# Three reduced-precision passes in place of full fp32 products, with operands split in two, in a fused attention and mixture-of-experts layer

## The reference

```python
x = L0_attn_hidden                                   # (4, 1024, 256)
x = x + attention(layernorm(x), Wq, Wk, Wv, Wo)      # window of 64 keys
x = x + ffn(layernorm(x), ...)

# ffn, xf = x as (4096, 256)
scores = sigmoid(xf @ gate_w.T + lb_bias)
topw, topi = top_k(scores, 2); topw /= topw.sum(-1) + 1e-8
for e in range(8):
    m = topi == e
    wmean = (topw * m).sum() / max(m.sum(), 1)
    y = (silu(xf @ gate[e].T) * (xf @ up[e].T)) @ down[e].T
    out += where(m.any(-1), y * wmean, 0)
out += (silu(x @ sgate.T) * (x @ sup.T)) @ sdown.T   # width 256, two halves
```

## Time and profile before

| what | value |
|---|---|
| median of 3 runs | 613.49 us (612.69 to 614.48) |
| profiled execution | 616.98 us, its span 615.2 us |
| PE busy | 555.0 us, 90% of the span |
| DVE, ACT, POOL busy | 354.0, 289.5, 218.4 us |
| chain that ended last, by engine | PE 71%, DVE 13%, an unknown queue 6%, ACT 4% |
| mean granted TensorE clock | 0.97 |

### The profile page before, as it was taken

How to read it: one execution, slowest core, us unless ns; L and a number is a source line. 1 busy time by engine, 2 the same in 40 slices (tenths; PEclk the granted TensorE clock), 3 DMA queues, 4 the chain that set the end, 5 groups by cost and what they waited for, 6 DMA issues and landing times.

```text
span 615.2 us, 14456 instructions
## 1 busy us (share of the span) xinstructions
PE 555.0 (90%) x4969; PEld 417.2 (68%) x4969; DVE 354.0 (58%) x1084; ACT 289.5 (47%) x650; POOL 218.4 (36%) x384
## 2 busy tenths in 40 slices
PE   7699999989898898898898987898999999999995
PEld 4466766666566565565575664786888887868884
DVE  4456577666465575675665567268555554533454
ACT  3366665645445555455455563221555554541110
POOL 4000012342240431422413423662456555555620
PEclk9899999999798998999999999698999999999999
DMA  7400000210201101112101101115455554518753
GB/s 249 164 3 3 2 2 4 62 45 20 63 23 40 52 20 55 37 27 63 36 2 38 36 2 38 70 57 159 135 152 162 153 159 134 157 58 301 247 147 126
DMA packets 37862, 50.79 MB, mean 83 GB/s; under 512 B 9244, under 2 KB 28063, under 8 KB 37792
## 3 DMA queue, kind: packets, MB, share of 16 engines
q1 hardware_dynamic: 31264, 33.02, 17.7%
q0 software_dynamic: 6528, 16.86, 8.3%
HBM read 27.36 MB, written 23.27 MB: 82 GB/s over the span
## 4 chain that ended last, share of the span: by engine, by line
PE 71%; DVE 13%; another core or an unknown queue 6%; ACT 4%; issue 3%; DMA 2%; POOL 1%; DVEq 0%; SPq 0%; POOLq 0%; ACTq 0%
PE ps L774 10%; PE ps L694 7%; PE ps L525 6%; PE ps L491 5%; PE ps L791 5%; PE ps L576 5%; PE ps L511 5%; PE ps L501 4%; DVE rmax L997 4%; PE ps L704 3%; PE ps L554 3%; PE ps L562 3%; PE ps L536 3%; PE ps L766 2%
## 5 line engine op out<-in xcount | busy, mean ns | idle before, releaser
L997 DVE TRANSPOSE_TENSOR_REDUCE rmax<-ps 128x32 f32<-128x1024 f32 x64 | 79.5, 1242 | 62.8 <-PE ps L525 61.0
L459 POOL DMA_INDIRECT y_rows<-vm,dest x72 | 70.2, 976 | 63.5 <-issue 40.1
L367 POOL TENSOR_TENSOR rstd<-mv,epsb 128x2 f32<-128x2 f32 x32 | 6.2, 193 | 241.6 <-DVE mv L982 241.6
L868 ACT ACTIVATE probs<-ps 128x1024 f32<-128x1024 f32 x64 | 65.7, 1026 | 25.0 <-PE ps L541 25.0
L774 PE MATMUL ps<-wF,wA 128*128 x288 | 75.0, 383 | 0.5 <-DVE wA L1246 0.5
L422 POOL DMA_INDIRECT z_slots<-z,slot x64 | 64.7, 1011 | 29.4 <-issue 18.0
L525 PE MATMUL ps<-bd,kT 64*128 64x256 f32 x512 | 66.4, 380 | 0.0
L694 PE MATMUL ps<-zT,wF 128*128 128x256 f32 x256 | 62.4, 388 | 0.6 <-ACT vm L957 0.6
L874 ACT COPY pvs<-ps 128x256 f32<-128x256 f32 x64 | 23.8, 372 | 81.5 <-remote 42.5
L694 PEld LDWEIGHTS ps<-zT,wF 128*128 128x128 f32 x256 | 49.5, 195 | 7.8 <-ACT vm L957 1.0
L525 PEld LDWEIGHTS ps<-bd,kT 64*128 64x128 f32 x512 | 50.0, 191 | 5.0
(11 more groups left out here) (160 smaller groups left out, 1095.5 us busy)
## 6 DMA issues: line engine op xcount, KB each, us to landing
z<-z_slots SPq DMA_DIRECT2D x72, 129.0 KB
bd<-y_rows SPq DMA_DIRECT2D x8, 512.0 KB, 7.4
out<-xs SPq DMA_DIRECT2D x16, 256.0 KB, 3.6
wF<-wffn SPq DMA_DIRECT2D x10, 384.0 KB, 3.3
xs<-x SPq DMA_DIRECT2D x7, 512.0 KB, 6.0
shift<-negs SPq DMA_DIRECT2D x128, 2.0 KB
z<-y_rows SPq DMA_DIRECT2D x4, 512.0 KB, 6.7
probs<-y_rows SPq DMA_DIRECT2D x4, 512.0 KB, 7.5
```

What stands on the lines that cost most here:

```text
L459: eng.indirect_dma_start(y_rows, bass.IndirectOffsetOnAxis(ap=dest[:, m:m + 1], axis=0), yo[:, m, :], None, bounds_check=K * T - 1, oob_is ...
L868: eng.activation(probs[:, n % 2, :], S[n % 2].rearrange("p a c -> p (a c)"), ACT.Exp, scale=HD ** -0.5).then_inc(s_P, 1)
L997: eng.tensor_reduce(rmax[:, n % 2, 0:32], S[n % 2].rearrange("p a (c q) -> p (a c) q", q=32), AX.X, ALU.max, apply_transpose=True).then_in ...
```

## The change

Every large product except `down` of the shared expert and the attention's inner products is made of three matmuls on operands of type fp32r, a 32-bit type that the matmul takes in reduced precision: hi x hi, hi x lo and lo x hi, where hi is the operand rounded to fp32r and lo the rest (`product`).

```diff
+                def product(out, lhsT, rhs, start, stop, skip=False):
+                    for n, (a, b) in enumerate(((0, 0), (0, 1), (1, 0))):
+                        mm = eng.matmul(out, lhsT(a), rhs(b), start=start and n == 0,
+                                        stop=stop and n == 2, skip_group_check=skip)
+                    return mm
```

```diff
-                    eng.tensor_copy(z1[:, m % 2, :], ps[:, 4 + m % 2, 0:D]).then_inc(s_z1, 1)
+                def rows_lo(t, q, m):
+                    eng.wait_ge(s_zh, t + 1)
+                    eng.tensor_tensor(z1[:, m % 2, 1, :], ps[:, 4 + m % 2, 0:D], f(z1[:, m % 2, 0, :]),
+                                      ALU.subtract).then_inc(s_zl, 1)
...
-                    chain(eng.tensor_tensor(table[0], const("tile").unsqueeze(2).to_broadcast([P, NTS, E]),
-                                           over_tiles(tiles_end), ALU.is_ge))
-                    chain(eng.tensor_reduce(tile_e[:, :], table[0], AX.X, ALU.add))
+                    chain(eng.tensor_scalar(fit, tiles_end, const("index"), None, ALU.is_le))
+                    chain(eng.tensor_reduce(e_col, fit, AX.X, ALU.add))
...
+                turn_of = [max(5 * g // 4 + 3, 2 * (g - GA) + 3) for g in range(NG)]
```

More of the change, by code:

```diff
@@ L294, in step @@
                             load_weights(g - 2)
+                        if n == 1 and old >= 2:
+                            store_zt(g - 2)
                 def prologue():
@@ L650, in step @@
                             yT_of(g + 2)
+                        if n == 0 and old >= 2:
+                            zT_of(g - 2, (place - 2) % GPB)
                         if project:
@@ L737, in epilogue @@
                     places_of(NG - 1)
+                    down(2)
+                    gate_up(5)
+                    eng.wait_ge(s_dg, 1)
+                    eng.matmul(ps[:, BANK_B, 64:64 + 2 * NTS], onesf[:, :], probs[:, 0, 64:64 + 2 * NTS],
+                               start=True, stop=True).then_inc(s_tb, 1)
+                    down(3)
                     gate_up(6)
@@ L790, in tile_down @@
                     after(eng, s_y1, t - 1)
[L791 to L792 removed]
+                    product(ps[:, 2 + m % 2, 0:D], lambda a: hT[:, m % 2, a, :],
+                            lambda b: weights(e, b, 4 * P, 6 * P), True, True).then_inc(s_d1, 1)
                 def tile(q, m, first, last):
@@ L1073, in step @@
                             normalise(1, g - 2, (place - 2) % GPB)
+                        if n == 1 and old == 3:
+                            comparisons(g - 3, last=False)
+                        if n == 3 and old:
+                            statistics(1, g - 1, (0,), False)
                         if ahead or n < BPG - 1:
@@ L1098, in step @@
                             normalise(1, g - 1, (place - 1) % GPB)
-                        if n == 2 and old:
-                            statistics(1, g - 1)
+                        if old or n:
+                            oT_lo(b - 1, (n - 1) % BPG)
+                        if n == 2 and g + 3 < NG:
+                            for c in range(2, XC) if old == 1 else ():
+                                eng.wait_ge(s_x[c], 16)
+                            statistics(0, g + 3, (0,), False)
                         if n == 3 and ahead and old >= 2:
```

516 lines of the change are left out of this document (333 added, 183 removed).

## The result

The changed kernel takes **633.4 us** (median of 4, 630.21 to 635.41) against 613.99 for the kernel before: ratio 1.031, 95% interval 1.026 to 1.036. It is slower by 3%, where 8% faster was forecast.

What follows compares the result with a forecast made beforehand. PE was taken to bound most of the kernel, apart from the sweep's unnamed hole and DVE's table in the epilogue. Terms -15 (tiles), -16 (sweep), -7.5 (epilogue), -11 (last stage) gave -49.5, from median 613.49 to 564 us; range 541 to 597.

Steps and rivals of the forecast that it cites:

- The unnamed hole: Sweep: ACT's unnamed wait while POOL scatters, 12 times, 42.5 us; taken as fixed, PE idling 0.3 us longer each.
- my own signs of being wrong: Whole kernel: a pass above 0.11 us, sweep steps that keep their length, or a growing hole in them.
- Tile stage: 72 tiles of three products: -15 us, from -23 to 0, a tile at 1.41 us.
- POOL runs without a gap and PE stalls: Rival, tile stage: a 1.35 us stall every four tiles, +24 us, so 588 us; chance 0.20.
- upper ends of my four terms: Worst cases of sweep (+15), tile stage (0), epilogue (-2) and last stage (-5).
- Price of a product: All 600 products: 0.327 us each instead of 0.432, saving 0.105 each, 63 us of PE time.
- slow pass: Rival, all 600 products: a product costs 0.648 us instead of 0.432, about 738 us in all; chance 0.08.
- Sweep: Sweep and prologue: -16 us, from -28 to +15; PE saves 1.66 us a step, a third lost to waits.
- DVE binds the sweep: Rival, sweep: it keeps its length, 0 instead of -16 us, so 580 us; chance 0.15.
- Epilogue: After the sweep: -7.5 us, from -10 to -2, by 44 cheaper products and a shorter DVE table.
- Last stage: Final stage: -11 us, from -12 to -5; 88 products save 9.2 us, three end additions becoming one save 1.8.

Runs made afterwards that it cites:

- e5: Kernel before with only its scatters' four indirect DMAs spread over four blocks; 587.36 us, ratio 0.958.
- e16: Kernel before, unaltered, profiled again; 613.02 us.
- e4: Changed kernel with each scatter's four indirect DMAs spread over four blocks; 577.27 us, ratio 0.937.
- e1: Changed kernel with one plain fp32 matmul on the hi parts in each product, lo parts made but unused; 625.56 us, ratio 1.019.
- e7: Changed kernel with the places and the scatter put ahead of the 1/std of y on POOL; 668.02 us.
- e12: e4 with a memset of 384 columns behind each tile-stage indirect DMA; 556.8 us beside a kernel before of 579.3 us.
- e2: Changed kernel with every indirect DMA replaced by a direct one of the same size to fixed rows, routing left out; 550.52 us.
- e3: Kernel before with every indirect DMA replaced by a direct one of the same size to fixed rows, routing left out; 578.62 us.
- e11: e4 with the first of PE's three table broadcasts moved behind a down and a gate_up in the epilogue; 575.62 us.
- e13: e12 with PE's last epilogue broadcast (tile weights) and DVE's copy of it moved behind the last down; 557.24 us beside 579.3 before.
- e17: e13 with a memset of 448 columns in place of 384; 560.43 us beside a kernel before of 578.8 us.
- e8: e4 with the tile stage's three products each one plain fp32 matmul of the hi parts; 565.08 us, ratio 0.920.
- e15: The kernel of e12 once more, beside a kernel before of about 614 us; 568.22 us, ratio 0.925.

## Why the prediction was wrong, by its own steps

**The unnamed hole (the step that failed).** I wrote that the hole in the sweep "is a fixed time" and that PE with less work idles longer in it, 0.3 us each. It costs 3.6 us a step before (24.45 against 20.87 in e5; 2.9 by e16's 23.75) and 5.3 us in the changed kernel (25.07 against 19.78 in e4). On twelve steps the difference is 20 us, or 29 by e16, where I had 4. Read at one clock (under e1) it has two parts. The first: at full clock the hold is worth 2.6 us before (23.45 against 20.87) and about 4.0 in the changed kernel (23.7 against 19.7), since the step does not shorten by what the passes save; nearly all of the 1.2 us becomes idle time and not 0.3. The scatter starts 10.15 us after the step in the changed kernel and in e1 alike, whatever a product costs, and in the kernel before at 9.3. So PE's products do not set when it starts, and the change has put 0.85 us on the way there, where I had 0.5. Which operation on that way does it was not shown; e7, which was to test it, did not. The second part is the clock, which my sum did not have at all: it fell in each of the changed kernel's nine steps, which makes 1.4 us a step on average, and in five of the kernel before's (two in e16), which makes 1.0 us (0.3). With it the sweep came out worse than without the change. I had put the hole down as something that the change leaves alone because its own rows, the indirect DMAs, are not touched. Of my own signs of being wrong all three came: a pass above 0.11, steps that keep their length, and PE's wait behind the hole, which grew from 22.3 to 39.0 us.

**Tile stage: the rival came.** "POOL runs without a gap and PE stalls" stood at +24 us for 0.20; the tile stage was to be at -15 + 24 = +9, and it is at +8.8. The place and the kind of stall were in the earlier trace rows; the chance was wrong. I set it against the sequencer that "keeps a tile above 1.4 us", but 1.42 us a tile is not enough: holds are still there at 1.58.

That the sum agrees to 0.2 us is luck. Against e12, which has no holds, they cost 19 us and not 24, and the base is not -15: without holds the stage is 108.3 us (e12) or 108.4 (e2), 10 less than the kernel before's and only 6 less than e3's 114.4. A tile takes 1.42 us, near my 1.41 but for the wrong reasons: a matmul is 0.119 us instead of 0.109, so nine of them and three transposes are 1.40, and the three REGISTER_ALU cost nothing visible. What I overlooked is that every eighth tile takes 2.1 to 2.3 us in e2 and in e12, always where PE's program loads the next eight expert numbers (`experts_of`); e3, whose kernel loads four at a time, has no tile over 1.9. No run changed this alone, so the cause is not shown.

**Two rivals from one cause.** I had kept the hole in the sweep and the stalls in the tile stage apart, one as a constant and one as a rival. Both go away with the same edit (e2) and come together. The upper ends of my four terms (+15, 0, -2, -5) add up to about 621 us, and to 645 with the stalls, and 633.4 lies between; I had cut the range at 597 because "not all come together". With one cause behind two of them they did.

**Price of a product.** 0.357 us where 0.327 was forecast: 45 us in all and not 63. The slow pass (0.648) did not come. My lower bound took the matmuls of the earlier trace rows to be at the lower clock, where the profile's window has 1.00, so it was no reading of a row. By an estimate from the Trainium skill ("FP8 and Floating Point Precision", TensorE Precision Notes: true FP32 is four passes) three passes would be 0.324; the row shows 0.357, so a reduced matmul of 256 columns is dearer than a quarter of the full product.

**Sweep without the hold.** -1.1 us a step had been forecast from 1.66 less a third for waits. The runs have 1.1 to 1.2 from 16 x 0.075 and no waits. "DVE binds the sweep" did not come: DVE is at 17.2 of 19.65 us in e2.

**Epilogue.** -7.5 became +5.5. Without indirect DMAs it is still +2.1 (51.9 against 49.8), so the holds are about 3.4 of it, as far as single executions tell: two of them stand in its chain in the changed kernel, the wait of 2.52 us and the 1.15 us of L672 below. For the rest, the table on DVE did get shorter, but PE must broadcast it in three pieces in its own order. Its chain in the changed kernel, where L810 and L823 are broadcasts:

```profile
400.11 2.52 another core or an unknown queue
...
419.54 1.15 PE ps L672
...
424.91 0.85 PE ps L810 x2
425.76 1.71 PE ps L773 x4
427.46 1.84 PE ps L530 x12
...
434.94 0.44 PE ps L823 x2
435.38 0.91 PE ps L773 x4
436.30 1.43 PE ps L530 x12
437.72 0.88 PE ps L773 x4
```

Before, the chain from 411 us on was DVE's alone; now it goes from DVE to PE and back, and ends in PE's own gate_ups and downs, the first of them at the lower clock (1.71 for a down in place of 0.87, 1.84 for a gate_up in place of 1.43; the granted clock is 0.52 from 424.9 to 428.4 us). Moving one broadcast (e11, e13, e17) did not clearly win anything back, so that the waits at the broadcasts make the 2.1 us is not shown.

**Last stage.** -9.8 where -11 was forecast: a pair is 2.30 us instead of 2.59, 22 x 0.29 = 6.4, and the rest is the shorter end, which e1 has too: with plain products its last stage is 3.5 us below the kernel before's. At 270 GB/s the chain of this stage still has no DMA in it.

**The version to keep.** e8 (565.1 us, 8.0% faster than the kernel before) leaves the lo parts out of the tile stage's products; e15 with all three passes is at 568.2, 7.5% faster. Both are mostly the spread scatter. Where no hold was, e12 is still 4% faster than the kernel before.

## What to carry to other kernels

An unnamed wait that comes with another engine's work is a suspect to be priced by a run, not a constant: ask what its length hangs on, and whether the engine that the change relieves sets the steps in which it stands. Making PE faster can bring everything else closer together, and in the sweep it was four indirect DMAs right behind each other that cost; spreading four of them over a step, a change of a few lines, gave 27 us before and 56 us after, more than the change of every product. And where one cause appears as two terms of a sum, their chances are not independent.

## What the runs showed of the hardware

- While indirect DMAs from POOL follow each other at 1.28 us, ACT and DVE stand for up to 3.9 us before work that PE has long finished (3.7 in the changed kernel). In the tile stage nearly no holds were seen at a steady 1.63 us with plain products; with three-pass products there were some at 1.58 and many at 1.47. Direct DMAs of the same size from the same queue did not do it. In two of eight groups of runs it was missing altogether, and the kernel before took 579 us instead of 614.
- A matmul of 256 columns on fp32r operands takes 0.119 us with its weight load (12 in 1.43 us), against 0.432 for a full fp32 product (4 in 1.73).
- The granted clock fell behind a hold in which PE had stood: 0.91 over eight steps with three-pass products, 1.00 with plain products in the same order (e1), though PE stood nearly as long there (34.3 us behind pv's copy in the whole run, against 39.0). A step of the changed kernel takes 24.7 us at 0.93 and 25.8 at 0.87.
